# Attention kernel: the output products of the last tiles dealt out singly over the slots of the last four steps, their buffers multiplied, and the gate factors computed one step later

## What is computed

```python
xn = layernorm(x)
# branch 1: causal linear attention; phi(t) = elu(t) + 1; q, k, v = phi(xn@wq), phi(xn@wk), xn@wv
o = num / den                     # running sums of k v^T and k over the rows before
y1 = o @ wo
# branch 2: softmax attention with normalised, scaled queries
h = softmax(q_scaled @ k.T / sqrt(32)) @ v
gates = softmax(h @ Wr.T + br)    # 15 routed heads, the top 3 kept, times 3
sw = softmax(h @ Ws.T + bs)       # 2 shared weights
gain = 2*sw[0]*sw.sum() + 2*sw[1]*sum(top3(gates))*3
y2 = (h * gain) @ Wp.T + bp
out = x + y1 + y2
```

## Time and profile before

| | us |
|---|---|
| median of 3 runs | 4469.12 |
| lowest, highest | 4468.86, 4476.95 |
| the profiled execution's own time | 4465.83 |
| its span in the trace | 4464.1 |
| PE busy in it | 4044.7 (91%) |
| DVE busy | 3402.0 (76%) |
| ACT busy | 2809.0 (63%) |
| POOL busy | 309.8 (7%) |
| mean granted PE clock, share of full | 0.967 |

### The profile page before, as it was taken

How to read it: one execution, slowest core, us unless ns; L and a number is a source line. 1 busy time by engine, 2 the same in 40 slices (tenths; PEclk the granted TensorE clock), 3 DMA queues, 4 the chain that set the end, 5 groups by cost and what they waited for, 6 DMA issues and landing times.

```text
span 4464.1 us, 88010 instructions
## 1 busy us (share of the span) xinstructions
PE 4044.7 (91%) x36076; PEld 1621.6 (36%) x36076; DVE 3402.0 (76%) x3542; ACT 2809.0 (63%) x3831; POOL 309.8 (7%) x210
## 2 busy tenths in 40 slices
PE   3389999999999999999999999999999999999888
PEld 1243333333333333333333333433333333333223
DVE  3647888887888877887887787788678777777874
ACT  3237767776766666666666666666666666666661
POOL 0100000000000000000000000000000000000001
PEclk7689999999999999999999999999999999999999
DMA  3421211112122222223222222212221221221224
GB/s 123 139 80 49 67 51 52 52 54 66 53 80 59 82 72 74 64 70 89 58 83 69 77 61 72 86 56 87 60 69 54 62 79 47 82 62 53 61 68 144
DMA packets 373143, 319.90 MB, mean 72 GB/s; under 512 B 160192, under 2 KB 320960, under 8 KB 372032
## 3 DMA queue, kind: packets, MB, share of 16 engines
q1 hardware_dynamic: 372672, 313.43, 23.9%
HBM read 237.30 MB, written 76.02 MB: 70 GB/s over the span
## 4 chain that ended last, share of the span: by engine, by line
issue 62%; PE 20%; ACT 6%; POOL 5%; DVE 4%; DMA 2%; SPq 0%; ACTq 0%; POOLq 0%; DVEq 0%
ACT prob L768 4%; PE ps L904 4%; PE ps L1016 4%; PE ps L1030 4%; POOL rn L616 3%; PE ps L994 2%; DVE acc L1510 1%; POOL y L603 1%; PE ps L912 1%; PE ps L947 1%; PE ps L968 1%; PE ps L864 1%; PE ps L970 1%; PE ps L929 1%; POOL rstd L599 0%
## 5 line engine op out<-in xcount | busy, mean ns | idle before, releaser
L768 ACT ACTIVATE prob<-ps 128x1024 f32<-128x1024 f32 x2048 | 1985.4, 1023 | 670.0 <-PE ps L1016 615.0
L1510 DVE TENSOR_TENSOR acc<-acc,prob 128x2048 f32<-128x2048 f32 x896 | 2051.6, 2290 | 53.4 <-ACT prob L768 36.1
L1030 PE MATMUL ps<-prob,v 128*32 128x512 f32 x8192 | 1107.1, 613 | 1.8 <-ACT prob L768 1.8
L1016 PE MATMUL ps<-q_hi,k_hi 32*128 32x512 f16 x4096 | 429.9, 388 | 198.0 <-ACT prob L768 159.6
L1016 PE MATMUL ps<-q_hi,k_lo 32*128 32x512 f16 x4096 | 420.4, 379 | 2.0 <-issue 2.0
L1016 PE MATMUL ps<-q_lo,k_hi 32*128 32x512 f16 x4096 | 419.9, 379 | 0.0
L904 PE MATMUL ps<-x_hi,w_hi 128*128 128x512 f16 x1024 | 397.1, 388 | 6.8 <-issue 4.5
L904 PE MATMUL ps<-x_lo,w_hi 128*128 128x512 f16 x1024 | 394.3, 385 | 0.0
L904 PE MATMUL ps<-x_hi,w_lo 128*128 128x512 f16 x1024 | 393.8, 385 | 0.0
L994 PE MATMUL ps<-wop_hi,fin 128*128 128x512 f16 x1024 | 334.8, 387 | 19.9 <-DMA fin<-olo_scratch 18.6
L1016 PEld LDWEIGHTS ps<-q_hi,k_hi 32*128 32x128 f16 x4096 | 110.1, 91 | 620.5 <-ACT prob L768 406.0
(11 more groups left out here) (250 smaller groups left out, 4559.2 us busy)
## 6 DMA issues: line engine op xcount, KB each, us to landing
x_hi<-xhi_scratch SPq DMA_DIRECT2D x64, 512.0 KB, 6.7
x_lo<-xlo_scratch SPq DMA_DIRECT2D x64, 512.0 KB, 7.9
x_in<-in_x SPq DMA_DIRECT2D x64, 256.0 KB, 7.3
rq<-rq_scratch SPq DMA_DIRECT2D x64, 256.0 KB
rdl<-rdl_scratch SPq DMA_DIRECT2D x64, 256.0 KB
rden<-rden_scratch SPq DMA_DIRECT2D x64, 256.0 KB
fin<-hhi_scratch SPq DMA_DIRECT2D x128, 128.0 KB, 2.4
fin<-hlo_scratch SPq DMA_DIRECT2D x128, 128.0 KB, 2.8
```

The costliest lines, as they stand in the source:

```text
L768: s_.activation(prob[i % 3][:, 2 * p:2 * p + 2, :], ps[:, 2 * p:2 * p + 2, :], ACT.Exp, bias=-SHIFT, scale=1.0 / CQK).then_inc(exped, 1)
L1016: last = t_.matmul(bank[h], kk[rows32(h), cols128(kt)], qq[rows32(h), :], start=(kk is kh and qq is qh), stop=(kk is kl and not wide))
L1030: last = t_.matmul(bank[OUT][rows32(h), :], v[m // NB % 2][:, kt, rows32(h)], prob[i % 3][:, h, :], start=(kt == 0), stop=(kt == TT - 1))
L1510: v_.tensor_tensor(acc[:], acc[:], prob[i % 3][:], ALU.add).then_inc(summed, 1)
```

## The change

The last stage from tile 44 on (L0) is a list of single products, o and h apart, dealt out one to each pair of slots, with o products ahead of the h products of their tiles. Steps 60 to 63 now hold 6, 7, 7 and 7 products (54 half products); the pair of slots (0, 2) is used too. 13 products, two of the four gates and the last block's division stay behind the last step, in the order FINAL. The products alternate between banks X0 and X1; product i waits until that of i - 2 is added. The loads of a product stand five slots ahead of it (LEAD). From tile 44 on there are 10 buffers y, in the memory of x_hi and x_lo, and 11 buffers fin, in that of w_hi and w_lo, both free by then; a buffer loaded for the gates is kept until the h product has used it, so that h from tile 48 on is loaded once. The load of y of a tile counts on the same semaphore as its o; a load into a used y waits for all late stores issued so far. The last block's division is made on 128 partitions out of PSUM, without the way through scratch memory. `gate_gains` of blocks 0 to 11 moves from slot 13 to slot 4 of the next step. One semaphore replaces six for DVE's waits on itself, and a few others are merged; these renamings are cut below.

```diff
-LATE = {LIGHT: (4, 8, 12), LIGHT + 1: (4,), LIGHT + 2: (4, 8, 12), LIGHT + 3: (4, 8, 12)}
+L0, G0 = N_FIRST, N_GATED * BT
+HALVES = [(0, 2)] + [(i, i + 1) for i in range(4, TT, 2)]
+LATE = (
+    [(kind, L0 + i) for i in range(3) for kind in "oh"],
+    [("o", L0 + 3), ("h", L0 + 3)] + [("o", G0 + i) for i in range(5)],
+    [("o", G0 + 5), ("o", G0 + 6)] + [("h", G0 + i) for i in range(4)] + [("o", G0 + 7)],
+    [("o", G0 + 8), ("o", G0 + 9)] + [("h", G0 + i) for i in range(4, 8)] + [("o", G0 + 10)],
+)
+FINAL = [("o", G0 + 11), ("total", None), ("o", G0 + 12), ("h", G0 + 8), ("h", G0 + 9), ("o", G0 + 13), ("h", G0 + 10), ("o", G0 + 14),
+         ("h", G0 + 11), ("o", G0 + 15), ("gates", B * NB - 1)] + [("h", G0 + i) for i in range(12, 16)]
+def late(s):
+    if not LIGHT <= s < LAST:
+        return []
+    return list(zip(LATE[s - LIGHT], HALVES[-len(LATE[s - LIGHT]):]))
...
             def load_y(t):
-                if t >= 2:
-                    sp.wait_ge(y_stored[t % 2], t // 2 * 16)
-                sp.dma_start(y[t % 2][:], x_d[t // TT, token_rows(t), :]).then_inc(y_loaded[t % 2], 16)
+                i, before = y_at(t), y_count(t) - 1
+                if before and t < L0 + NY:
+                    sp.wait_ge(y_stored[i], before * 16)
+                elif before:
+                    sp.wait_ge(y_late, late_stores[0] * 16)
+                sp.dma_start(y[i][:], x_d[t // TT, token_rows(t), :]
+                             ).then_inc(y_loaded[i] if t < L0 else fin_loaded[FIN_BUF[USE_AT["o", t]]], 16)
...
+                    if s >= LIGHT and kt == 13 and gate_after(s) is not None:
+                        for use in gate_uses(gate_after(s)):
+                            load_use(*use)
+                    for s1 in (s, s + 1):
+                        for pr, slots in late(s1):
+                            if (s1 - s) * TT + slots[0] - LEAD == kt:
+                                load_product(*pr)
+                    for s1 in (s - 1, s):
+                        for pr, slots in late(s1):
+                            if (s1 - s) * TT + slots[1] + 2 == kt and pr[0] == "h":
+                                store_y(pr[1])
+            for pr in FINAL:
+                if pr[0] == "o":
+                    load_product(*pr)
             store_h_hi(NBLK - 1)
             store_h_lo(NBLK - 1)
+            for use in gate_uses(B * NB - 1):
+                load_use(*use)
+            for t in range(NT - 2 * BT, NT):
+                store_y(t)
...
+            def late_product(pr, ks=range(KC)):
+                i = LATE_AT[pr]
+                if i >= 2 and ks[0] == 0:
+                    kind, t = LATE_PRODUCTS[i - 2]
+                    pe.wait_ge(yo_done if kind == "o" else y_done, t + 1)
+                branch((X0, X1)[i % 2], pr, "oh".index(pr[0]), ks)
...
+            pe.wait_ge(lg_kept, B * NB - 2)
+            gates(B * NB - 2, X2)
             weigh(NBLK - 1, TT - 1)
+            for pr in FINAL:
+                if pr[0] == "total":
+                    total(NBLK - 1, bank[0])
+                elif pr[0] == "gates":
+                    pe.wait_ge(lg_kept, pr[1])
+                    gates(pr[1], X2)
+                else:
+                    late_product(pr)
...
-                    if kt == gate_slot(s) + 2 and gate_block(s) is not None:
+                    if kt == gate_slot(s) + 2 and s >= LIGHT and gate_block(s) is not None:
                         gate_gains(gate_block(s))
...
                     if kt == 4 and n is not None:
                         scale_rn(n)
+                    if kt == 4 and s <= LIGHT and gate_block(s - 1) is not None:
+                        gate_gains(gate_block(s - 1))
                     if kt == 5 and mp is not None:
                         invert_den(mp)
...
+            add_late(LATE[-1][-1])
             add_up(NBLK - 1, TT - 1)
+            gate_logits(B * NB - 2)
+            add_late(FINAL[0])
+            dve.wait_ge(den_done, NBLK)
+            dve.wait_ge(hm_done, NBLK - 1)
+            v_.reciprocal(rden[:], bank[0]).then_inc(rden_done, 1)
+            dve.wait_ge(out_kept, NBLK)
+            dve.wait_ge(rden_done, NBLK)
+            v_.tensor_tensor(hm[:], hm[:], rden[:], ALU.mult).then_inc(hm_done, 1)
+            gate_gains(B * NB - 2)
+            add_late(FINAL[2])
             split_h(NBLK - 1)
+            for pr in FINAL[3:]:
+                if pr[0] == "gates":
+                    gate_logits(pr[1])
+                    gate_gains(pr[1])
+                else:
+                    add_late(pr)
```

More of the change, by code:

```diff
@@ L131, in n_gated, with gate_uses, y_at, y_count @@
     return sum(gate_block(i) is not None for i in range(FIRST, min(s, LAST)))
+def gate_uses(f):
+    return [("g", f * BT + j) for j in range(BT)]
 USES = []
[L136 removed]
+for s_ in range(FIRST, LIGHT):
     if gate_block(s_) is not None:
[L138 to L144, removed]
[L145 to L146 removed]
+        USES += gate_uses(gate_block(s_))
+    if out_tile(s_) is not None:
+        USES += [("o", out_tile(s_)), ("h", out_tile(s_))]
+N_EARLY = len(USES)
+for s_ in range(LIGHT, LAST):
+    USES += [pr for pr, slots in late(s_) if slots[0] < gate_slot(s_)]
+    if gate_block(s_) is not None:
+        USES += gate_uses(gate_block(s_))
+    USES += [pr for pr, slots in late(s_) if slots[0] >= gate_slot(s_)]
+USES += gate_uses(B * NB - 2)
+for kind_, i_ in FINAL:
+    USES += gate_uses(i_) if kind_ == "gates" else [] if kind_ == "total" else [(kind_, i_)]
+USE_AT = {use: i for i, use in enumerate(USES)}
+NFIN_LATE = NFIN + 6
+FIN_BUF, FIN_PREV, FIN_LOADS = [], [], []
+for u_, (kind_, t_) in enumerate(USES):
+    if kind_ == "h" and t_ >= G0:
+        b_ = FIN_BUF[USE_AT["g", t_]]
+        prev_, loads_ = None, FIN_LOADS[USE_AT["g", t_]]
+    else:
+        held = [FIN_BUF[USE_AT["g", i]] for i in range(G0, NT) if USE_AT["g", i] < u_ < USE_AT["h", i]]
+        used = {b: max([i for i in range(u_) if FIN_BUF[i] == b], default=-1) for b in range(NFIN if u_ < N_EARLY else NFIN_LATE)
+                if b not in held}
+        b_ = min(used, key=lambda b: used[b])
+        prev_ = used[b_] if used[b_] >= 0 else None
+        loads_ = max([FIN_LOADS[i] for i in range(u_) if FIN_BUF[i] == b_], default=0) + (3 if kind_ == "o" and t_ >= L0 else 2)
+    FIN_BUF.append(b_), FIN_PREV.append(prev_), FIN_LOADS.append(loads_)
+NY = 10
+def y_at(t):
+    return t % 2 if t < L0 else (t - L0) % NY
+def y_count(t):
+    return sum(y_at(i) == y_at(t) for i in range(t + 1))
 def build(nc, x_d, w6_d, wop_d, wg_d, bqkv_d, bp_d, bg_d, temp_d, qe_d, out_d):
@@ L213, in build @@
         y = [sb(f"y{i}", [P, D]) for i in range(2)]
+        late_w, late_x = cursor_w, cursor_w + 2 * size([P, 6, KC, P], F16)
+        fin += [at(f"fin{i}", [P, 2, KC, P], F16, late_w + (i - NFIN) * 2 * KB) for i in range(NFIN, NFIN_LATE)]
+        y += [at(f"y{i}", [P, D], F32, late_x + (i - 2) * 2 * KB) for i in range(2, NY)]
         NZ = NL + TOP
@@ L467, in _ @@
                             pack(rdl_c, rdl_d, rdl, dl_out, dl_in, p)
-                        if f is not None:
-                            for j in range(BT):
-                                load_use("g", f * BT + j)
+                        if f is not None and s < LIGHT:
+                            for use in gate_uses(f):
+                                load_use(*use)
                         if o is not None:
@@ L1570, in step @@
                 for kt in range(TT):
+                    for s1 in (s - 1, s):
+                        for pr, slots in late(s1):
+                            if (s1 - s) * TT + slots[1] + 1 == kt:
+                                add_late(pr)
                     if kt == 0 and p is not None:
```

367 lines of the change are left out of this document (159 added, 208 removed).

## The result

| | before | after |
|---|---|---|
| median, us | 4471.66 (4 runs) | 4412.57 (4 runs) |
| lowest, highest | 4468.86, 4476.95 | 4399.69, 4421.50 |
| the profiled execution's own time | 4465.83 | 4410.36 |
| its span | 4464.1 | 4408.6 |
| PE busy | 4044.7 | 4025.7 (91%) |

The account below looks back on a forecast made before the run. Bounds: load waits in steps 60 to 63, stores and loads through two y buffers in the tail, DVE saturated in the middle's late slots. Gains of 14.2, 29.7 and 0 took 4469.1 to 4425.2, say 4425 us; range 4413 to 4438.

Parts of the forecast that it names:

- Part 1: Steps 60 to 63: load waits go (16.5 us), 14 more half slots cost 2.8; a gain of 14.2 us.
- Rival A: Late transfers in the tail's burst of reads and part of the steps 60 to 63 gain lost: 4435 us, chance 0.15.
- the first wait of the tail: Before tile 59's o product, PE waits 1.8 us for y, whose load waits for all late stores.
- Part 2: The tail behind the last half product of step 63: a gain of 29.7 us, clock fall included.
- T: Time at which PE ends the last half product of step 63: 4387.3 before, near 4373 forecast.
- (d): In the tail, a clock fall behind the wait for tile 59's y: 2 us taken, bounds 0 and 5.
- (b): In the tail, the last division and the way of h through memory are covered by 7 us of products.
- Part 3: Gate factors moved out of slot 13 in steps 15 to 59: comes to 0, between +3 and -8 us.
- the three borders: Ends of steps 47, 51, 59: 1.2 us waits go, perhaps clock falls too; 1.8 us taken, bounds 0 and 10.
- the eight other steps: Gate steps with low clock in slots 13 and 14 behind the add of o: PE itself last, nothing gained.
- C: Rival: two-buffer waits and three border falls all go, no fall in the tail; 4417 us, chance 0.08.
- D: Rival: moved factors bring waits and clock falls in slot 8 of up to 12 next steps; 4498 us, chance 0.03.

Follow-up runs that it names:

- the mended tail: Changed kernel with tile 59's loads issued in slot 13 of step 63 and tile 60's add ahead of the factors: 4406.65 us, ratio 0.9861.
- the seven and the three profiles: Steps 15 to 59 unchanged in seven kernels with the factors in slot 4, 2919.9 us, and three with them in slot 13, 2930.9 us (means).

## Why the prediction was right in parts 1 and 2 and wrong in part 3

**Part 1, right.** -15.2 against -14.2. The slots of steps 60 to 63 take 3.16 us, no load is waited for, and steps 60 to 63 read 198.9 to 199.2 us in nine of the ten profiles with the change's five slots of lead, 199.6 in the tenth. Of the 1.0 beyond it 0.6 is in slot 0 of step 60, which belongs to the border. Where I wrote that this holds "if no load is late", the kernel with one slot of lead gives the price: 41 us. Rival A, transfers that come late, did not happen in any profile of the changed kernel. The latency of 2 us that the Trainium skill gives at high load (DMA: Bandwidth & Descriptors, Latency and other measured facts), by which my estimate made the first wait of the tail 1.8 us longer, isn't seen here: the store landed after 3.16 and the load after 2.79 us.

**Part 2, right, down to its steps.** T is 4361.3 (4373 was forecast; the steps ahead are shorter by what Part 3 missed). The wait for y is 1.80 us (1.8 forecast), the reciprocal of 512 columns 3.37 (3.3), hm ends at T + 12.0 (11.8), the add of tile 60 at T + 15.1 (14.5), PE's wait for it is 2.07 (1.5), h is stored at T + 15.7 (15.3). Gates of block 15 end at T + 33.7 (31.3), since that second wait is longer and the clock fell at its end; the end is T + 47.3 (45.1 + 2). The fall came at the second wait, not behind the first as (d) had it, and its 3.4 us cost the 2 that were taken for it. Which wait brings it isn't fixed: with the same tail it stands behind the first in three profiles and at the second in four. The cover in (b) was put at 7 us and is some 9, by the loads' landing and by the two kernels with the loads held back. One sentence of (b) is too wide: the division's way through memory is covered, but a later division delays the add of tile 60 behind it on DVE, and that one PE does wait for. Taking the factors out from between them won part of the 3.9 us in the mended tail.

**Part 3, wrong in one term.** The prediction put the waits at 5.4 us won and 7.2 lost, and the clock at 1.8 won "of bounds 0 and 10", so 0 in all. Measured, in the profiles put together: 5.4 us of waits added where 7.2 were expected (in the first profile step 16 has none, the others 0.4 to 1.3), all waits together 2.7 us less where 1.8 more were expected, and the clock, as PE busy for the same work, 8.4 us less where 1.8 were taken. That makes -11.0 by the profiles; the move alone is -16.5 (-11 to -23) by the times. The clock's 1.8 us is the step that failed; it measured 8.4. It was mis-sized at one point of the reasoning: I counted falls only at the three borders whose wait went away whole, and wrote of the eight other steps that "nothing is gained" since PE itself is the last there. For the waits that is nearly true, for the clock it is false. In these eight steps, from slot 11 to slot 1 of the next step, PE waits 46.7 us in place of 49.1 (means of the seven and the three profiles), but the low clock is 50.7 in place of 66.0 and PE is busy for 6.5 us less; in the four others, with the mask and the three borders, it is busy for 2.9 less. In the profile after, steps 35, 39 and 43 have 3.4 us less of low clock and step 55 none of its 6.8, although their wait for the add of o stands. Step 55, before and after (PEclk is the third number from the end):

```profile
3895.00:3921.00 26.00, 21.61 (x162) 8.40 (x154) 19.33 (x26) 12.97 (x19) 0.00 (x0) 0.87 0.06 18
```

```profile
3888.00:3912.00 24.00, 19.24 (x178) 7.64 (x174) 18.45 (x17) 13.59 (x19) 0.00 (x0) 1.00 0.07 20
```

By what way eleven instructions less on DVE do this in the eight steps isn't shown. Shorter waits behind slot 13 would be the obvious answer, and these steps don't bear it out: the scores' wait in slot 15 was 1.64, 1.79 and 2.02 us in steps 35, 39 and 55 before and is 2.24, 2.22 and 2.16 after. The 8.4 us lie inside the bounds of 0 and 10, but by luck: the bounds were the price of the three borders, and two thirds of the gain came from the steps left out.

The rule of the Trainium skill that I weighed there (TensorE: Matmul & The Clock Gate, Part 1, the throttled state is the default and activity releases it) pointed to a gain. The rows agree with its direction, with one exception: what took waits out of slots 12 to 15 took low clock with it (from 91.0 us to 65.3, then to 47.8 and 37.5), and what put longer ones in brought it back (61.4); but with the factors in slot 2 the low clock was 75.1 us at the same waits in these slots and fewer in all.

**Rivals.** C, more than forecast, came nearest in size, its 4417 being 4.4 us over the time, but not as it was told: step 47's low level stayed at 6.8 us, those of steps 51 and 59 fell by half, and the tail had its fall. Its 6.4 us don't follow either: by its own bounds three border falls are 10 less the 1.8 already taken, 8.2, which gives 4415. A gain of the clock deserved more than 0.08, since the rows had more to lose than three borders: a low level stood in slots 13 to 15 of eleven of the twelve gate steps, and behind the start of slot 15 in seven of them. D, slower by falls in slot 8 of the next steps, did not happen: the added waits in slots 6 to 8 left the clock at its full level there, but for one fall in one of seven profiles.

**What isn't settled.** Steps 0 to 14, which no kernel changed, read 901.7 to 907.5 us in the fourteen profiles, the stretch ahead of step 0 reads 329.5 to 343.8, and the medians of 4 or 5 runs scatter by several us; of the 59 us a few may be that, and the 0.4 us by which the time lies outside the range is less than it. That a given wait brings a fall, and of what length, can't be said from these runs: the same wait of the same kernel had a low level of 3.4 us in one profile and of 6.8 in another. That moving the factors lowers the low clock and PE's busy time is shown, by doing it alone and by undoing it. That the waits are the way isn't: no experiment held the waits and changed the clock alone, the two go together only in the sums, and the kernel with the factors in slot 2 goes against it.

## What to carry to other kernels

Where PE is over 90% busy and waits in a burst, price a wait as itself plus up to half of the time at the low clock behind it (here 25.7 us less of low clock gave 8.4), and count the falls of every place with such a burst, not only of those where a wait vanishes whole. Work that nobody needs yet, on an engine that is saturated for a few slots, is worth moving to the next idle stretch even if it costs a little there: moving more of it, and further, was worth another 16 us, most of it in waits. An order written by hand needs its loads ahead of the queue's own waits, not only a landing time ahead of their use: one slot of lead hid a transfer of 2.8 us on paper and cost 41 us.

## What the runs showed of the hardware

A reciprocal on DVE of 128 x 512 took 3.37 us: with 203 ns for 8 columns and 933 for 128 it lies on the straight line of 6.1 ns a column (933 + 384 x 6.1 = 3275), 0.1 us above it. Waits of nearly the same length don't bring falls of the same length. At the end of step 59 the kernel before has a low level of 6.8 us in its first profile and of 3.4 in its second. The waits there are 1.18 us in the one and 1.19 in the other, and then these, first profile first:

```profile
4169.37 0.61 PE L1016 MATMUL ps<-q_hi,k_hi 32*128 32x512 f16 x4 [2.57 <-issue]
```

```profile
4179.69 0.40 PE L1016 MATMUL ps<-q_hi,k_hi 32*128 32x512 f16 x4 [2.61 <-issue]
```
